# Second attention of a two-layer decoder: one TensorE stretch for maxima and scores, and a new order of the steps around it

## What is computed

```python
x = x + _L0_xattn_ref(_layernorm(x), ctx_1024, ctx_1024, ...)   # 16 heads of 64
x = x + _L0_ffn_ref(_layernorm(x), kernel, bias, a, b)          # one 128x128 product, with bias
x = x + _L1_xattn_ref(_layernorm(x), ctx_1024, ctx_1024, mask_1x1xSxS2_ik0, ...)   # 16 heads of 8
x = x + _L1_ffn_ref(_layernorm(x), w_gate, w_up, w_down)        # quantised weights and rows

def _L1_xattn_ref(Q, K, V, mask, ...):
    ...
    scores = jnp.einsum('bhqd,bhkd->bhqk', q, k) / jnp.sqrt(jnp.float32(DK))
    scores = jnp.where(mask == 0, jnp.float32(-1000000000.0), scores)
    attn = jax.nn.softmax(scores, axis=-1)
    out = jnp.einsum('bhqk,bhkd->bqhd', attn, v)
    return out @ Wo_w + Wo_b
```

## Time and profile before

| | |
|---|---|
| time, median of 3 runs | 714.21 us (713.11 to 714.27) |
| the profiled execution, its time | 713.85 us |
| its span in the profile | 712.1 us |
| PE busy in the span | 679.0 us |
| DVE, POOL, ACT busy | 523.9, 435.2, 401.1 us |
| granted TensorE clock, mean | 0.995 |

### The profile page before, as it was taken

How to read it: one execution, slowest core, us unless ns; L and a number is a source line. 1 busy time by engine, 2 the same in 40 slices (tenths; PEclk the granted TensorE clock), 3 DMA queues, 4 the chain that set the end, 5 groups by cost and what they waited for, 6 DMA issues and landing times.

```text
span 712.1 us, 23629 instructions
## 1 busy us (share of the span) xinstructions
PE 679.0 (95%) x9273; PEld 572.8 (80%) x9273; DVE 523.9 (74%) x1607; ACT 401.1 (56%) x902; POOL 435.2 (61%) x572
## 2 busy tenths in 40 slices
PE   8999999999999999999999989999999999998785
PEld 7787898888988888888888978788888888885444
DVE  5867668568668478676666666778887878778996
ACT  2534463563644644536445444565766666766896
POOL 3597577477488378478477524555655646642775
PEclk9999999999999999999999999999999999999999
DMA  9511101201100210110210120000000000000011
GB/s 266 131 40 36 38 1 39 66 3 46 37 18 23 67 29 18 37 31 2 67 32 2 32 79 7 11 7 7 11 6 7 6 4 9 0 2 1 24 45 53
DMA packets 26767, 23.84 MB, mean 33 GB/s; under 512 B 7148, under 2 KB 23356, under 8 KB 26680
## 3 DMA queue, kind: packets, MB, share of 16 engines
q1 hardware_dynamic: 25864, 22.25, 11.3%
q10 hardware_dynamic: 816, 0.36, 0.2%
HBM read 10.25 MB, written 2.10 MB: 17 GB/s over the span
## 4 chain that ended last, share of the span: by engine, by line
PE 86%; DVE 8%; issue 3%; ACT 2%; POOL 0%; ACTq 0%; DVEq 0%; POOLq 0%
PE bank L1339 9%; PE bank L1313 8%; PE bank L1359 8%; PE bank L1201 6%; PE bank L2005 6%; PE bank L1203 4%; PE bank L1202 4%; PE bank L2038 4%; PE bank L1350 4%; PE bank L1321 4%; PE bank L1252 3%; PE bank L2023 2%; PE bank L1263 2%; PE bank L1364 2%; DVE f_h_max L2255 2%
## 5 line engine op out<-in xcount | busy, mean ns | idle before, releaser
L748 POOL TENSOR_TENSOR a_turned<-a_turned,a_rope 128x512 f32<-128x512 f32 x63 | 81.6, 1295 | 19.1 <-DVE a_turned L864 19.1
L749 POOL TENSOR_TENSOR a_qr<-a_straight,a_turned 128x512 f32<-128x512 f32 x64 | 81.7, 1278 | 4.9
L1072 ACT CAST a_qb<-a_qr 128x512 bf16<-128x512 f32 x64 | 38.6, 638 | 68.8 <-POOL a_qr L749 68.8
L760 POOL TENSOR_TENSOR a_k_turned<-a_k_turned,a_rope 128x308 f32<-128x308 f32 x61 | 48.0, 787 | 34.5 <-DVE a_k_turned L874 34.1
L1339 PE MATMUL bank<-a_vs,a_probs 77*64 77x65 f32 x2048 | 66.8, 223 | 0.0
L1339 PEld LDWEIGHTS bank<-a_vs,a_probs 77*64 77x64 f32 x2048 | 62.5, 137 | 5.0 <-issue 2.4
L1084 ACT COPY a_fold<-bank 112x128 bf16<-112x128 bf16 x31 | 8.3, 266 | 101.5 <-PE bank L1276 101.5
L1359 PE MATMUL bank<-a_wo,a_oTn 128*128 128x128 f32 x512 | 62.4, 275 | 0.0
L1359 PEld LDWEIGHTS bank<-a_wo,a_oTn 128*128 128x128 f32 x512 | 60.9, 192 | 1.5
L927 DVE TENSOR_REDUCE a_am<-bank 128x6 bf16<-128x462 f32 (+1 forms) x96 | 50.0, 578 | 14.2 <-PE bank L1263 14.2
L1313 PE MATMUL bank<-a_qr,a_kr 64*77 64x128 f32 x960 | 59.4, 273 | 0.0
(11 more groups left out here) (291 smaller groups left out, 1989.7 us busy)
## 6 DMA issues: line engine op xcount, KB each, us to landing
a_vs<-a_stage SPq DMA_DIRECT2D x16, 312.8 KB
out<-x_all SPq DMA_DIRECT2D x16, 128.0 KB, 1.8
x_all<-in_x_dram SPq DMA_DIRECT2D x7, 256.0 KB, 6.4
a_vs<-a_stage SPq DMA_DIRECT2D x4, 308.8 KB
a_mask_in<-in_mask SPq DMA_DIRECT2D x16, 77.0 KB, 4.1
a_wv<-in_ctx SPq DMA_DIRECT2D x16, 77.0 KB
a_ctx_in<-in_ctx SPq DMA_DIRECT2D x8, 128.0 KB
a_vs<-a_stage SPq DMA_DIRECT2D x4, 211.2 KB
```

The costliest lines, as they stand in the source:

```text
L748: steps.link(nc.gpsimd.tensor_tensor(tv, tv, rope[:, 1:2, :].broadcast_to([128, 4, S]), ALU.mult))
L749: nc.gpsimd.tensor_tensor(qr[P][:, 2 * k:2 * k + 2, :, :].rearrange("p t j s -> p (t j) s"), sv, tv, ALU.subtract if made else ALU.add).th ...
L760: steps.link(nc.gpsimd.tensor_tensor(tv, tv, rope[:, 3:4, 0:KL].broadcast_to([128, 4, KL]), ALU.mult))
```

## The change

- PE computes the maxima products and the f32 scores of sequence `b+1` in one stretch, `maxima_and_scores(b+1)`, in slot `b` before `values(b)`. The two kinds alternate, so that one uses feature rows 0 to 63 while the other uses 64 to 127. Before, the scores stood at the start of slot `b+1`. The first sequence keeps both apart (`first_maxima`, `first_scores`).
- PE's order in a slot is new, and the four rows of the last feed-forward part (L395) move from the fourth slot to the third. j=0: transposes, rows of the last feed-forward part (third slot), folds, turn_out, queries_keys, out_projection, the stretch, values, ffn_turn, turn_maxima. j=1: values_rows, folds, turn_out, ffn_project, out_projection, the stretch, values, turn_maxima. So `ffn_project` moves from the end of the j=0 slot into the middle of the j=1 slot, and `values_rows` to its start.
- DVE: `ffn_residual` and `statistics` move behind the front's steps, just ahead of `residual`. `start.rows` and `normalised_rows` move behind `maxima`. The last step of `maxima` is a reduction over one tensor that holds both parts, instead of a maximum of two tensors.
- ACT: the two copies of `transposed` are one; the exponentials come in the order 2, 1, 0, the first ahead of `turned_out`; `ffn_turned` moves to the start of the j=1 slot, ahead of `fold_in`; `rows_in` moves to the third slot, ahead of `keys_in`.
- POOL: `ffn_bias` moves behind `out_bias` and `spread_keys`.

The core of the diff:

```diff
@@ -1516,15 +1516,16 @@
     keysb = [part(spent[n], 0, [D, 2, 5 * 128], BF16) for n in ("wk", "k_turned")]
-    xT = part(spent["wk"], 640, [D, 2 * S])
+    turned = sb("turned", [D, 2 * S + 2 * KL], F32)
+    xT, ctxT = turned[:, 0:2 * S], turned[:, 2 * S:]
...
-    max_m, max_r = sb("max_m", [S, H1], F32), sb("max_r", [S, H1], F32)
+    parts = sb("max_parts", [S, 2, H1], F32)
     row_max = am[:, CROW:FOLD]
@@ -1602,7 +1603,7 @@
         last = isinstance(prev, int) and prev == PAIRS // 2 - 3
-        return turn(P, j, prev, 1 if last else 3)
+        return turn(P, j, prev, 1 if last else 2)
@@ -1687,10 +1688,11 @@
                 start.deviation(pool, p + 2)
-                ffn_bias(p + 2)
             if j == 0 and more:
...
                 spread_keys(p + 1, 1 - P)
+            if j == 0 and more_pre(p):
+                ffn_bias(p + 2)
             if j == 1 and more_pre(p):
@@ -1734,11 +1736,11 @@
                 dve.wait_ge(x_full[i], b + 1)
-                steps.did(nc.vector.tensor_reduce(max_m[:, 8 * i:8 * i + 8],
+                steps.did(nc.vector.tensor_reduce(parts[:, 0, 8 * i:8 * i + 8],
                                                   px[i][:].rearrange("p (h k) -> p h k", k=KM), AX, ALU.max))
             dve.wait_ge(x_full[2], b + 1)
-            steps.link(nc.vector.tensor_reduce(max_r[:], pr[:, 0:256].rearrange("p (h k) -> p h k", k=RPAD), AX, ALU.max))
-            nc.vector.tensor_tensor(row_max, max_m[:], max_r[:], ALU.max).then_inc(maxima_ready, 1)
+            steps.link(nc.vector.tensor_reduce(parts[:, 1, :], pr[:, 0:256].rearrange("p (h k) -> p h k", k=RPAD), AX, ALU.max))
+            nc.vector.tensor_reduce(row_max, parts[:].rearrange("p a h -> p h a"), AX, ALU.max).then_inc(maxima_ready, 1)
...
-            if j == 1 and more_pre(p):
-                ffn_residual(p + 2)
-                statistics(p + 2)
             if turn(P, j, g, 0):
@@ -1796,8 +1795,6 @@
                 front.row_steps(steps, prev)
-            if j == 0 and more_pre(p):
-                start.rows(dve, steps, p + 2)
             if pair(p, 0):
@@ -1809,16 +1806,22 @@
                 front.weighted_steps(steps, 0, B - 2 * front.G)
+            if j == 1 and more_pre(p):
+                ffn_residual(p + 2)
+            if j == 1 and more_pre(p):
+                statistics(p + 2)
             if not first:
...
                 residual(b - 1)
+            if j == 0 or more:
+                maxima(b + 1)
+            if turn(P, j, g, 1):
+                front.variances(steps)
+            if j == 0 and more_pre(p):
+                start.rows(dve, steps, p + 2)
             if j == 1 and more_pre(p):
                 normalised_rows(p + 2)
-            if turn(P, j, g, 1):
-                front.variances(steps)
-            if j == 0 or more:
-                maxima(b + 1)
             if turn(P, j, g, 3):
@@ -1835,8 +1838,7 @@
             act.wait_ge(a_turned, p + 1)
-            nc.scalar.copy(xT[:], pa[:, 0:2 * S])
-            nc.scalar.copy(ctxT[:], pa[:, 2 * S:2 * S + 2 * KL]).then_inc(turned_in, 1)
+            nc.scalar.copy(turned[:], pa[:, 0:2 * S + 2 * KL]).then_inc(turned_in, 1)
@@ -1868,8 +1870,8 @@
-        def exps(b):
-            for g in (2, 0, 1):
+        def exps(b, gs):
+            for g in gs:
                 act.wait_ge(s_full[g], b + 1)
@@ -1901,17 +1903,20 @@
             first = isinstance(b, int) and b == 0
+            if j == 1 and more_pre(p):
+                ffn_turned(p + 2)
             fold_in(b)
...
                 cast_keys(p + 1, 1 - P, 0)
+            exps(b, (2,))
             if not first:
                 turned_out(b - 1)
-            exps(b)
+            exps(b, (1, 0))
+            if back(P, j, prev) and j == 0:
+                front.rows_in(act, prev, pm)
             if j == 0:
-                if more_pre(p):
-                    ffn_turned(p + 2)
                 if more:
@@ -1924,7 +1929,7 @@
                 cast_keys(p + 1, 1 - P, 1)
-            if back(P, j, prev):
+            if back(P, j, prev) and j == 1:
                 front.rows_in(act, prev, pm)
@@ -1966,11 +1971,8 @@
-        def score_maxima(b, p, P, j, first):
+        def masks_under(b):
             pe.wait_ge(maxima_ready, b)
-            if not first:
-                out_projection(b - 2)
-
             pe.wait_ge(s_free[2], b)
...
@@ -1997,27 +2003,52 @@
-        def scores(b, P, j):
...
+        def score(P, j, g, i, half, tile, first):
+            return nc.tensor.matmul(SCORES[g][:, i * S:(i + 1) * S], keys[P][FEATURES[half], j, 128 * tile:128 * tile + 128],
+                                    q1[P][FEATURES[half], j, :], start=first, stop=False, skip_group_check=True)
+
+        def maxima_and_scores(b, p, P, j):
+            lo, hi = FEATURES
+            masks_under(b)
+            pe.wait_ge(cast_done[j], p + 1)
+            nc.tensor.matmul(pr[:, 0:128], q1b[P][lo, j, :], keysb[P][lo, j, 512:640],
+                             start=False, stop=True, skip_group_check=True)
+            nc.tensor.matmul(px[1][:], q1b[P][hi, j, :], keysb[P][hi, j, 0:512],
+                             start=False, stop=True, skip_group_check=True).then_inc(x_full[1], 1)
+            score(P, j, 2, 0, 0, 4, False).then_inc(half_done, 1)
+            pe.wait_ge(s_free[1], b)
+            score(P, j, 1, 0, 1, 0, True)
+            nc.tensor.matmul(px[0][:], q1b[P][lo, j, :], keysb[P][lo, j, 0:512],
+                             start=False, stop=True, skip_group_check=True).then_inc(x_full[0], 1)
+            score(P, j, 1, 1, 1, 1, False)
+            pe.wait_ge(s_free[0], b)
+            score(P, j, 0, 0, 0, 0, True)
+
+            pe.wait_ge(half_done, b + 2)
+            nc.tensor.matmul(pr[:, 128:256], q1b[P][hi, j, :], keysb[P][hi, j, 512:640],
+                             start=False, stop=True, skip_group_check=True)
+            score(P, j, 2, 1, 1, 4, False).then_inc(x_full[2], 1)
+            for i in (1, 2, 3):
+                score(P, j, 0, i, 0, i, False)
+                if i < 3:
+                    score(P, j, 1, i + 1, 1, i + 1, False)
+
...
             pe.wait_ge(fold_ready, b + 1)
-            for g in (2, 0, 1):
+            for g in (2, 1, 0):
                 tiles = range(4 * g, 4 * g + (4 if g < 2 else 2))
@@ -2094,32 +2125,33 @@
         pe.wait_ge(setup, 11)
-        score_maxima(0, 0, 0, 0, True)
+        first_maxima()
         yield
         turn_maxima(0)
+        first_scores()
...
                 transposes(p + 1, 1 - P)
-            scores(b, P, j)
+            if back(P, j, prev) and j == 0:
+                pe.wait_ge(f_done, p + 2)
+                front.rows(pe, prev, pm)
+            if j == 1 and more:
+                values_rows(p + 1)
+            folds(b)
             if not first:
                 turn_out(b - 1)
-            folds(b)
-            if j == 0:
-                score_maxima(b + 1, p, P, 1, first)
-            elif more:
-                score_maxima(b + 1, p + 1, 1 - P, 0, False)
-            else:
-                out_projection(b - 1)
-            if pair(p, 1) and j == 0:
-                pe.wait_ge(front.means_read, 1)
-            if j == 0 and more_pre(p):
-                ffn_turn(p + 2)
             if j == 0 and more:
                 queries_keys(p + 1)
-            if j == 1 and more:
-                values_rows(p + 1)
+            if j == 1 and more_pre(p):
+                ffn_project(p + 2)
+            if not first:
+                out_projection(b - 1)
+            if j == 0:
+                maxima_and_scores(b + 1, p, P, 1)
+            elif more:
+                maxima_and_scores(b + 1, p + 1, 1 - P, 0)
             if pair(p, PAIRS - 1) and j == 0:
@@ -2130,11 +2162,15 @@
                 front.turn_sums(pe, pm)
-            if back(P, j, prev):
-                pe.wait_ge(f_done, p + 3 if more_pre(p) else PAIRS)
+            if back(P, j, prev) and j == 1:
+                pe.wait_ge(f_done, PAIRS)
                 front.rows(pe, prev, pm)
             if j == 0 and more_pre(p):
-                ffn_project(p + 2)
+                if pair(p, 1):
+                    pe.wait_ge(front.means_read, 1)
+                if back(P, j, prev):
+                    pe.wait_ge(front.xqT_ready, prev + 1)
+                ffn_turn(p + 2)
             if j == 0 or more:
```

27 lines of the change are left out of this document (14 added, 13 removed).

## The result

| | before | after |
|---|---|---|
| median, 6 runs each on one chip | 714.08 us | 719.38 us (717.14 to 722.63) |
| the profiled execution, its span | 713.85, 712.1 us | 717.14, 715.4 us |
| mean of a loop iteration | 25.99 us | 27.01 us |
| the four pairs ahead of the loop | 51.66 us | 50.96 us |

The ratio of after to before is 1.0082, 95% interval 1.0061 to 1.0104: slower. The kernel after ran once more beside later experiments: 718.21 us, ratio 1.0067 (1.0046 to 1.0087). Each experiment's ratio is to runs of the kernel before made beside it (their medians are 713.1 to 714.4 us), and the ratios leave out four single executions far above the others of their kernel (from 3% longer up to nearly five times as long).

The account below looks back on a forecast made before the run. PE was taken to bound the kernel before; afterwards DVE's rows, held by POOL, make it wait. Loop 5.0 us slower, first pairs 0.7 and end 1.1 saved: 714.21 + 3.2 = 717.4 us, range 710.0 to 721.0.

Parts of the forecast that it names:

- stretch of maxima and scores: PE's maxima products and scores: 1.58 us together instead of 1.77, bounds 1.48 to 1.77.
- first slot: Odd slot: 6.3 us without contention, 0.35 more as POOL's spreading from 3.5 to 6.2 holds start.rows; 6.7.
- second: Even slot: PE's product, then DVE's chain to the normalised rows, 6.5 us, plus 0.07 for variances.
- third: Odd slot: POOL spreads keys until 6.7 us and holds start.rows, 0.85 more, 7.25 us.
- fourth: Even slot: 2.4 us to the feed-forward product, then 4.1 on DVE before the next transposes, 6.5 us.
- the four pairs ahead of it: Pairs before the loop: 12.7 us against 12.82, four save 0.4 us, and the first 0.3 more.
- 1.32 less 0.4 that fold_in then shows: End of the stage: slot 31 has no scores before the folds; with values earlier by 0.2, 1.1 us saved.
- No collision: Rival: POOL doesn't hold DVE's rows; iteration 25.8 us, 3.7 us faster, 710.5 us; chance 0.22.
- Gains and losses meet: Rival: third slot's collision costs 0.3 us instead of 0.85, iteration 26.4, no change in time; chance 0.17.
- PE stays the bound: Rival: DVE's chain and rows are shorter; 0.35 us saved in each of 32 slots, 703 us; chance 0.05.
- Worse collisions: Rival: odd slots lose 0.85 us each, even ones 0.2; iteration 27.9, 9.6 us slower, 724 us; chance 0.06.
- the moved POOL bias: POOL's ffn_bias behind the spreading: costs nothing, as POOL has 11 us of air an iteration.

Follow-up runs that it names:

- e6: Kernel after with half of the large spreading instruction left out (keys of four heads instead of eight, output wrong): 712.94 us, ratio 0.9989.
- e4: Kernel after with the last step of the maxima again a maximum of two tensors: 722.20 us, ratio 1.0117.
- e8: Kernel before with only the new last step of the maxima, a reduction over one tensor: 713.56 us, ratio 0.9996.
- e5: Kernel after with start.rows back ahead of residual and POOL's ffn_bias back ahead of out_bias and spread_keys: 709.73 us, ratio 0.9953.
- e2: Kernel after with ffn_project ahead of the folds in the j=1 slot: 717.53 us, ratio 1.0057.
- e3: Kernel after with start.rows ahead of residual and ffn_project ahead of the folds: 716.62 us, ratio 1.0046.
- e9: Kernel after with only POOL's ffn_bias back ahead of out_bias and spread_keys: 740.89 us, ratio 1.0374.
- e7: Kernel after with the edits of e5 and e2, and in j=1 slots turn_out ahead of folds and normalised_rows ahead of maxima: 711.74 us, ratio 0.9976.
- e1: Kernel after with only start.rows back ahead of residual and the maxima: 716.33 us, ratio 1.0040.
- e10: e5 with the order of e7 in the second slot of an iteration alone: 708.07 us, ratio 0.9929.

## Why the prediction was right, and where its working was not

**The answer.** 717.4 us were predicted, and slower as the likeliest; 719.38 and 718.21 were measured. The interval of the ratio lies wholly above 1. The forecast was 3.2 us slower, the medians say 5.3 and 4.9. The mechanism held: POOL's instructions hold `tensor_scalar` rows that stand beside them, and the rows set when PE goes on. e6 shows the first part at the place named (less POOL work, 0.8 us off the third slot), e4 and e8 that the form of the maxima's last step matters only in the new order.

**Slots** (a chain of sums against starts in the trace):

| | predicted | measured |
|---|---|---|
| stretch of maxima and scores | 1.58 | 1.54 |
| first slot | 6.7 | 6.40 |
| second | 6.57 | 6.85 |
| third | 7.25 | 7.11 |
| fourth | 6.5 | 6.67 |
| iteration | 27.0 | 27.01 |

The third slot went by its steps: keys spread from 3.9 us (4.0 predicted) to 6.6 (6.7), rows from 5.2 (5.3) to 6.7 (6.8). In the first, spreading ran from 3.2 to 5.9 us instead of 3.5 to 6.2: POOL got the statistics at 1.8 and not at 2.15, as DVE's front reduction (L367) began before the slot and not with it. In the second I was 0.28 short: statistics and residual took 1.85 us, not 1.67, `variances` 0.18 and not 0.07, and from the rows to the transposes it was 0.23 where I had 0.04 for a semaphore; the feed-forward product and the rows were each 0.1 shorter. Those 0.23 us are the loop's: from the last row to the transposes it is 0.23 to 0.25 us in it and 0.05 behind it (629.98). The fourth slot is reckoned 0.17 too short, in part by the same wait. That the sum is exact is luck: 0.3 and 0.14 too much in the first and third slots meet 0.28 and 0.17 too little in the others.

**The ends were mis-sized.** The loop was to cost 5.0 us and cost 5.0; the four pairs ahead of it were to save 0.7 and saved 0.70. But the end was to save 1.1 and saved 0.2 (from the last transposes to the end 85.59 before, 85.37 after), and the time from the first transposes to the second ones, to which the prediction gave nothing, grew by 0.44 us (11.65, 12.09). The failed term is "1.32 less 0.4 that fold_in then shows". The scores of the last slot are not gone: every sequence has its scores once, and those of the first now stand ahead of slot 0. And `fold_in` shows twice in the last two slots, not once: 1.4 us in all where 0.4 was put down. Waits of after from 640 to 660 us, and the longer of the two in the chain, where ACT's `rows_in` (L400) stands ahead of `fold_in` (L1871):

```profile
PE bank L2054 <- ACT a_qr L1871: 1.4, 2, 1.0
```

```profile
642.41 0.69 ACT a_qb L400
...
643.12 0.27 ACT a_qr L1871
...
643.43 0.73 PE bank L2054 x10
```

So the stage lost 5.0 - 0.7 - 0.2 + 0.4 = 4.5 us, not 3.2. The profiled executions differ by 3.3 because the one of before started the stage 1.25 us late, with a half-clock stretch that after's has not (below). The medians differ by 5.3 and, in the second comparison, by 4.9; what of that is above 4.5 isn't settled. The runs of after spread more (717.14 to 722.63), and the two slowest have the lowest granted clock (0.988 at 722.63, 0.993 at 720.78, against 0.997 at 717.14), but 719.21 has 0.997 too, and in the second comparison after did not spread more.

**The rivals.** No collision (710.5): in e5, without one in the loop, the time was 709.7, but with POOL gated and the rows ahead, not in the order of after; in that order e6 comes nearest, with 26.02 us an iteration against the rival's 25.8. Gains and losses meet: no, the third slot's collision cost 0.8 us and not 0.3. PE stays the bound: no, 2 us of an iteration are waits. Worse collisions (724): in after the value spreading held the rows of the even slots only in two of the pairs ahead of the loop (0.72 and 0.73 us for two instead of 0.59); in the loop it did so in e2, e3 and e9 (0.77) and in e7 (0.83), not in after.

**What the prediction didn't see.** It read L248's place in the order as free ("the moved POOL bias: nothing, ACT's air hides them"). In the trace of before L248 is what keeps POOL away from L236, by 1.3 us of waiting a pair. The four orders, by iteration in us, all with PE's new order:

| | ffn_bias first | ffn_bias last |
|---|---|---|
| start.rows ahead of residual | 25.56 (e5) | 26.61 (e1) |
| start.rows behind maxima | 28.3 or more (e9) | 27.01 (after) |

The bias's move can't be judged alone: with the rows late it must be last, with the rows early it must be first. The rows are better early in both columns, by 0.40 us and by 2.7 or more. The change took the worse of the two pairs that fit. In PE's own work the stretch gave what was predicted (0.2 to 0.4 us a slot): it takes 1.54 us where its two parts took 1.77. An iteration falls only from 25.99 to 25.56 in e5 and 25.27 in e10, that is 0.1 and 0.2 us a slot, with waits left in the even slots. No run has the stretch, or ACT's new order, without the rest of the change, so what each is worth by itself stays open.
